# Fields divided 24 to 15 over full banks, sums over positions on VectorE, the context term in one pass

## The reference

```python
def _cin_layer(x0, xk, W, b):
    out = jnp.einsum('bhd,bmd,shm->bsd', xk, x0, W) + b[None, :, None]
    return jax.nn.relu(out)
e = jnp.stack([tbl_0[ids[:, 0]], ..., tbl_38[ids[:, 38]]], axis=1)
x1 = _cin_layer(e, e, W1, b1)          # (1024, 128, 16)
x2 = _cin_layer(e, x1, W2, b2)         # (1024, 128, 16)
z = jnp.concatenate([x1.sum(axis=-1), x2.sum(axis=-1)], axis=-1)
h = jnp.concatenate([z, dense_ctx], axis=1)          # 128 + 128 + 16 = 272
h = jnp.maximum(h @ W_top1 + b_top1, 0.0)            # 512
h = jnp.maximum(h @ W_top2 + b_top2, 0.0)            # 256
y = h @ W_top3
```

## Time and profile before

| | us |
|---|---|
| median of 3 runs | 1210.94 (1210.28 to 1210.98) |
| the profiled execution | 1209.32 |
| its span | 1207.3 |
| TensorE busy | 1162.2 |
| VectorE busy | 1075.3 |
| GpSimd busy | 900.6 |
| ScalarE busy | 692.3 |

### The profile page before, as it was taken

The page is one execution under the profiler, slowest core; times in us unless marked ns, Lnnn a source line. Parts: engine busy times, 40 slices in busy tenths (PEclk is TensorE's granted clock), DMA queues, the critical chain, the costliest instruction groups (busy, mean ns, idle before and its releaser), DMA issues.

```text
span 1207.3 us, 18938 instructions
## 1 busy us (share of the span) xinstructions
PE 1162.2 (96%) x4952; PEld 898.9 (74%) x4952; DVE 1075.3 (89%) x3811; ACT 692.3 (57%) x2177; POOL 900.6 (75%) x930
## 2 busy tenths in 40 slices
PE   3897999999999999999999999999999999999998
PEld 2575777777777777777777677777778777777766
DVE  4476899999999999999999779999999999999966
ACT  3554565656666556666565555566666566656432
POOL 7898998888888888888887676888876454645432
PEclk9998999999999999999999999999999999999998
DMA  5111111111111111111111100111110000000000
GB/s 180 8 7 7 7 8 6 7 6 7 6 7 8 7 6 7 6 6 7 7 7 6 6 5 5 7 7 7 7 6 2 1 1 1 1 1 1 1 1 1
DMA packets 170249, 11.58 MB, mean 10 GB/s; under 512 B 163630, under 2 KB 169262, under 8 KB 170013
## 3 DMA queue, kind: packets, MB, share of 16 engines
q1 hardware_dynamic: 159901, 7.73, 7.5%
q0 software_dynamic: 10240, 2.64, 2.8%
HBM read 7.92 MB, written 0.00 MB: 7 GB/s over the span
## 4 chain that ended last, share of the span: by engine, by line
PE 59%; DVE 16%; ACT 12%; issue 6%; POOL 6%; DMA 0%; POOLq 0%; DVEq 0%; ACTq 0%; SPq 0%
PE ps L881 16%; PE ps L882 15%; DVE acc L769 15%; PE ps L885 14%; ACT fy L552 9%; POOL looked L422 4%; PE ps L914 3%; PE ps L837 2%; ACT ps L585 2%; ACT zh L584 1%; PE ps L850 1%; PE ps L851 1%; PE ps L853 1%; PE ps L825 1%; POOL fsum L431 1%
## 5 line engine op out<-in xcount | busy, mean ns | idle before, releaser
L769 DVE SCALAR_TENSOR_TENSOR acc<-ps,e,acc 128x128 f32<-128x128 f32 x3186 | 846.9, 342 | 76.6 <-PE ps L885 70.6
L431 POOL TENSOR_TENSOR fy<-fy 128x512 f32<-128x512 f32 (+1 forms) x256 | 403.0, 1574 | 204.7 <-ACT fy L552 196.3
L881 PE MATMUL ps<-w2h,x1h 128*128 128x512 f32 (+1 forms) x1280 | 523.3, 409 | 21.2 <-ACT fy L552 9.9
L882 PE MATMUL ps<-w2l,x1h 128*128 128x512 f32 (+1 forms) x1280 | 496.3, 388 | 0.0
L885 PE MATMUL ps<-w2h,x1l 128*128 128x512 f32 (+1 forms) x1280 | 495.5, 387 | 0.4 <-DVE x1l L721 0.4
L552 ACT ACTIVATE fy<-ps,e 128x128 f32<-128x128 f32 x1536 | 415.8, 387 | 83.0 <-PE ps L885 82.9
L422 POOL DMA_INDIRECT looked<-in_table,rows x320 | 311.6, 974 | 58.3 <-POOL fy L431 23.4
L881 PEld LDWEIGHTS ps<-w2h,x1h 128*128 128x128 f32 x1280 | 241.5, 189 | 125.9 <-DVE acc L769 33.9
L885 PEld LDWEIGHTS ps<-w2h,x1l 128*128 128x128 f32 x1280 | 241.1, 188 | 49.6 <-DVE x1l L721 0.9
L882 PEld LDWEIGHTS ps<-w2l,x1h 128*128 128x128 f32 x1280 | 241.7, 189 | 43.7 <-issue 4.7
L584 ACT ACTIVATE zh<-ps 128x512 fp32r<-128x512 f32 x168 | 103.7, 617 | 247.2 <-PE ps L837 243.2
(11 more groups left out here) (87 smaller groups left out, 624.4 us busy)
## 6 DMA issues: line engine op xcount, KB each, us to landing
e<-looked SPq DMA_DIRECT2D x360, 5.0 KB, 1.9
looked<-in_table,rows POOLq DMA_INDIRECT x320, 2.4
e<-looked SPq DMA_DIRECT2D x120, 4.5 KB, 1.9
w_st<-in_w SPq DMA_DIRECT2D x1, 1728.0 KB, 10.1
wt_sb<-in_wt SPq DMA_DIRECT2D x2, 512.0 KB, 4.1
w_st<-in_w SPq DMA_DIRECT2D x1, 768.0 KB, 5.9
w_sb<-in_w1a SPq DMA_DIRECT2D x1, 448.0 KB, 3.2
w1b_sb<-in_w1b SPq DMA_DIRECT2D x1, 448.0 KB, 3.9
```

The source lines that it names most:

```text
L431: nc.gpsimd.tensor_tensor(out, a, b, ALU.add).then_inc(s_fsum, 1)
L769: nc.vector.scalar_tensor_tensor(acc[:, sub, :] if m < fields("D", last)[-1] else y, y, emb(p, sub, m), acc[:, sub, :] if m else fsum[:, p ...
L881: nc.tensor.matmul(y, x1h[:, t % 2, at], w2h[:, cols], start=True, stop=False)
L882: nc.tensor.matmul(y, x1h[:, t % 2, at], w2l[:, cols], start=False, stop=False)
```

## The change

VectorE gets 24 fields in six full banks, ScalarE 15 in four banks, the last with three fields. The ten slots of a pair become D A D D A D D A D A. GpSimd's adds of a pair go from six of 256, 1024, 512, 512, 512 and 256 elements per partition to six of 256, 1024, 1024, 768, 512 and 256. The sum over positions becomes one VectorE instruction per tile, behind `first_layer_low`. The context's term gets its high and low parts stacked on 80 rows, so that one matmul of the fast fp32 form takes the place of one in plain fp32; ScalarE and VectorE prepare the parts once. Tiles 4 and 5 join those whose first layer is unsplit (SOON), pairs 4 to 6 those that add `fsum` at their end (LATE), fewer lookups are issued in pairs 0 to 5, and `e_hl` has four places instead of eight.

```diff
-SOON = 4
+SOON = 6
-MA = 12
+MA = 15
-ORDER = "DDADDADDAD"
+ORDER = "DADDADDADA"
-LATE = 4
+LATE = 7
-ADDS_PER_PAIR = A_BANKS + 3
-LAST_ADDS = 4
+ADDS_PER_PAIR = A_BANKS + 2
+LAST_ADDS = 2
...
 def lookups(p):
-    return 7 if p < 6 else 6
+    return 6 if p == 0 or p >= 4 else 5
 def high_slots(p):
-    return (6, 7) if p == 0 else (0, 1) if SPLIT_IN[p] < SOON else (3, 6)
+    return (6, 7) if p == 0 else (4, 5) if p == 2 else (1, 4) if SPLIT_IN[p] < SOON else (3, 6)
...
-        P1_OPS = 4
+        P1_OPS = 1
...
+                def middle_fields(p, j):
+                    added(p, j, j, fy[:, p % 2, :, 0:4, :], fy[:, p % 2, :, 0:4, :], fy[:, p % 2, :, MB * j:MB * (j + 1), :])
+                def last_fields(p):
+                    added(p, 3, 3, fy[:, p % 2, :, 0:3, :], fy[:, p % 2, :, 0:3, :], fy[:, p % 2, :, 12:MA, :])
+                def four_to_two(p):
+                    added(p, 4, 3, fy[:, p % 2, :, 0:2, :], fy[:, p % 2, :, 0:2, :], fy[:, p % 2, :, 2:4, :])
...
-                    added(p, 5, 2, fsum[:, p % 2, :, :], fy[:, p % 2, :, 0, :], fy[:, p % 2, :, 1, :])
+                    added(p, 5, 3, fsum[:, p % 2, :, :], fy[:, p % 2, :, 0, :], fy[:, p % 2, :, 1, :])
...
+                    if p == 2:
                         low_parts(nc.gpsimd, mine)
                     if then < PAIRS:
-                        four_to_two(then, 2, 1, 0)
+                        middle_fields(then, 1)
+                    look_ahead(1)
...
+                def context_low():
+                    rows = slice(CTX_ROWS[1], CTX_ROWS[1] + CTX)
+                    dve.wait_ge(s_ctxh, 1)
+                    nc.vector.tensor_tensor(ctx_r[rows, :], ctx_sb[rows, :], ctx_r[rows, :], ALU.subtract).then_inc(s_ctxl, 1)
...
+                def position_sum(t):
+                    nc.vector.tensor_reduce(p1[:, t * BT:(t + 1) * BT], x1[:, t % 2, :].rearrange("p (x r) -> p r x", r=BT),
+                                            mybir.AxisListType.X, ALU.add).then_inc(s_p1, 1)
...
                             first_layer_low(p // 2 + 1)
+                            position_sum(p // 2 + 1)
...
-                                 (wt1c_sb[:, f], ctx_sb[:, lo:hi])]
+                                 (wt1c_r[:, f], ctx_r[:, lo:hi])]
```

More of the change, by code:

```diff
@@ L18 @@
 CTX = 16
+CTX_ROWS = (0, 32, 64)
+CTX_K = CTX_ROWS[-1] + CTX
 F1, F2 = 512, 256
@@ L98, in bank_order @@
     slots = [[("A", 0, 0), ("D", 0, 0), ("A", 0, 1), ("D", 0, 1), ("A", 0, 2)]]
-    first = (("D", 0, 2), ("D", 0, 3), ("A", 1, 0), ("D", 0, 4), ("D", 0, 5), ("A", 1, 1), ("D", 0, 6), ("A", 1, 2), ("A", 2, 0))
-    slots += [[bank] for bank in first] + [[]]
+    slots += [[("D", 0, 2)], [("A", 0, 3)], [("D", 0, 3)], [("A", 1, 0)], [("D", 0, 4)], [("A", 1, 1)], [("D", 0, 5)], [("A", 1, 2)],
+              [("A", 1, 3)], [("A", 2, 0)]]
     for p in range(1, PAIRS):
@@ L245, in cin_tower @@
         prod = sb("prod", [P, LOOKED, ZP * DT])
-        e_hl = sb("e_hl", [P, LOOKED, P, DT])
+        e_hl = sb("e_hl", [P, HELD, P, DT])
         x0t = sb("x0t", [P, 2, N], F32R)
@@ L463, in last_sum @@
                     nc.gpsimd.tensor_tensor(fy[:, h, :, 0:2, :], fy[:, h, :, 0:2, :], fy[:, h, :, 2:4, :], ALU.add).then_inc(s_fsum, 1)
-                    pool.wait_ge(s_fy, last_count(1))
+                    pool.wait_ge(s_stt, stt_count(p - 1, 0))
                     pool.wait_ge(s_fsum, n + 1)
[L466 to L470, removed]
-                    nc.gpsimd.tensor_tensor(fsum[:, h, :, :], fy[:, h, :, 0, :], fy[:, h, :, 1, :], ALU.add).then_inc(s_fsum, 1)
[L473 to L481, removed]
+                    nc.gpsimd.tensor_tensor(fsum[:, h, :, :], fy[:, h, :, 0, :], fy[:, h, :, 1, :], ALU.add).then_inc(s_fsum, 1)
                 pool.wait_ge(s_rows, 1)
@@ L531, in _ @@
                         whole_sum(then)
-                    if p % 2 == 0 and p // 2 + 1 < TILES:
-                        position_sum(p // 2 + 1)
                     look_ahead(1)
@@ L618, in products_high, with context_high @@
                     for row in (ZH, ZW):
-                        nc.scalar.activation(e_hl[:, t % LOOKED, row:row + ZP, :].bitcast(F32R), src, ACT.Copy).then_inc(s_eh, 1)
+                        nc.scalar.activation(e_hl[:, t % HELD, row:row + ZP, :].bitcast(F32R), src, ACT.Copy).then_inc(s_eh, 1)
+                def context_high():
+                    act.wait_ge(s_mlpw, 16 * len(mlp_weights))
+                    nc.scalar.activation(ctx_r[:], ctx_sb[:], ACT.Copy).then_inc(s_ctxh, 1)
+                    nc.scalar.activation(wt1c_r[:], wt1c_sb[:], ACT.Copy).then_inc(s_ctxh, 1)
                 def sums_turned(t):
@@ L717, in square_low, with context_weights_low @@
                     nc.vector.tensor_tensor(zl[:, k % 2, :], ps[:, BK_T, :], zh[:, k % 2, :], ALU.subtract).then_inc(s_zl, 1)
+                def context_low():
+                    rows = slice(CTX_ROWS[1], CTX_ROWS[1] + CTX)
+                    dve.wait_ge(s_ctxh, 1)
+                    nc.vector.tensor_tensor(ctx_r[rows, :], ctx_sb[rows, :], ctx_r[rows, :], ALU.subtract).then_inc(s_ctxl, 1)
+                def context_weights_low():
+                    rows = slice(CTX_ROWS[2], CTX_ROWS[2] + CTX)
+                    dve.wait_ge(s_ctxh, 2)
+                    nc.vector.tensor_tensor(wt1c_r[rows, :], wt1c_sb[rows, :], wt1c_r[rows, :], ALU.subtract).then_inc(s_ctxl, 1)
                 def first_layer_low(t):
@@ L825, in turn @@
                         mm = nc.tensor.transpose(ps[:, BK_T, d * P:(d + 1) * P],
[L826 removed]
+                                                 e_hl[:, t % HELD, :, d], ident_sb[:])
                     mm.then_inc(s_full, 1)
@@ L957, in _ @@
                     nc.tensor.matmul(ps[:, TAIL_1[c], 0:n], wt1_sb[:, 0, f], p1[:, lo:hi], start=True, stop=False)
-                    nc.tensor.matmul(ps[:, TAIL_1[c], 0:n], wt1c_sb[:, f], ctx_sb[:, lo:hi], start=False, stop=False)
+                    nc.tensor.matmul(ps[:, TAIL_1[c], 0:n], wt1c_r[:, f], ctx_r[:, lo:hi], start=False, stop=False)
                 sums(TILES - 1)
@@ L1025 @@
     first_row = np.repeat(first_row.reshape(LOOKUPS, Q).T, BT, axis=0)
+    wt1c, ctx_t = np.zeros((CTX_K, F1), np.float32), np.zeros((CTX_K, B), np.float32)
+    for row in CTX_ROWS:
+        wt1c[row:row + CTX], ctx_t[row:row + CTX] = x["W_top1"][2 * S:], x["dense_ctx"].T
     arrays = {
```

62 lines of the change are left out of this document (33 added, 29 removed).

## The result

The changed kernel takes **1283.09 us** (median of four runs, 1282.56 to 1284.29), beside 1210.96 for the kernel before: a ratio of 1.0597 (95% interval 1.0579 to 1.0615). The forecast was 1243, at most 1258. The direction was right, the size was not: the loss is 72 us, where 32 were forecast.

The account below looks back on a forecast made before the run. VectorE and TensorE were both taken as near the bound, with a loop through GpSimd's adds closing after the change. 1209.3 + 42 + 0.5 - 7 - 2.3 - 1.2 = 1241.3, median 1.6 above: 1243 us; range 1208 to 1258.

Parts of the forecast that it names:

- The loop: Slot 3 to slot 3 through GpSimd's adds, `fsum` and VectorE's first bank: tiles of 37.4 us, +53 - 11 = +42.
- fixed part: Loop's share outside TensorE's slots 3 to 7: A bank, ScalarE, GpSimd 6.17, VectorE 2.16, hand-overs; 11.6 us a pair.
- the late add: Even pair's add before the 768 add, its bank drained late: next add starts at 10.9 instead of 10.4, 0.5 us.
- four of seven: Small network's steps at tile 17 that fill the loop's wait; the loop grows by 8 only, not 19: -11.
- Late tiles: Tiles without lookups: a 1.3 us wait in the even pair gives 34.65 a tile against 34.56; +0.5 in all.
- The term sized 0.65: VectorE's reduction over positions, one instruction a tile: 0.65 us, between 0 and 1.4.
- Early pairs: TensorE's 7.44 us standstill in pair 2 shrinks: 9 back, 2 paid for tiles 4 and 5; -7, between -10 and 0.
- Context: Eight plain fp32 products become one pass each: -2.3 in the late tiles, another 2.5 inside the loop's sum.
- Tail: The last add waited for seven fields on ScalarE; four fields in slot 1 are now early: -1.2 us.
- VectorE's relief going to TensorE: Rival: the sums arrive in time, tiles of 34.7 or at best 33.4 us, 1160 to 1192 in all; 15%.
- The loop closed only in part: Rival: the 768 add is cheap (1.30) and the even pair's lag absent: 1221, down to 1209; 12%.
- The clock rival: Rival: each wait of some 2 us at slot 3 draws a stretch at 1.2 GHz, 70 more, 1313; 3%.

Follow-up runs that it names:

- the context's trial: Kernel before with only the context's term in one pass of the fast fp32 form (`e_hl` in four places): 1203.16 us, ratio 0.9947.
- the three edits: Changed kernel, last three adds without lookups between them, `x1l` behind VectorE's third bank, sum over positions at the even pair's end: 1203.24 us, 0.9948.
- the fastest version: Changed kernel with the three edits, TensorE's sums in slot 3 instead of 5, and the last square's low part behind the pair's last bank: 1196.34 us, 0.9890.
- the order of slots: Changed kernel with ORDER = DADDADADDA, fourth A bank in slot 6: 1253.88 us alone, 1229.2 with the three edits.
- the late `fsum`: Changed kernel with LATE = 62, so pairs up to 61 add `fsum` at their end: 1266.72 us, ratio 1.0477.
- the early copy: TensorE's sums of the tile before in slot 3 instead of 5: 1287.76 us on the changed kernel, 1202.15 with the three edits.

## Why the prediction was wrong in size

**The loop (+42, measured +68).** The mechanism and its fixed part were right: 6.15 for GpSimd's chain, odd pairs 17.99. What failed is the step "in an even one three matmuls with the transposes 1.09, two matmuls 0.46, the sums 0.25: 7.3". It gave TensorE's work between slots 3 and 7 and no wait in it. Measured it is 8.77, and two waits stand there: line 866 waits for `x1l`, and line 859 for ScalarE's copy of the sums. The front said that `x1l` "stood in the same place, behind the fourth D bank". By D banks that is true; by slots it is one later, since the fourth D bank moved from slot 4 to slot 5, next to the step that needs `x1l`. So 19 ordinary tiles between pairs 7 and 49 grew by 67.6 us, 3.56 each instead of 2.5, which is 20 of the 26 missed. Of the 1.06 that such a tile is too long on average, putting `x1l` ahead gave back 0.6. With it away the fourth bank still comes some 0.2 later than the late add would let it, by the wait for the copy. The context's parts, priced at 0, are another 0.1: they make the two tiles of pairs 16 to 19 longer by 2.0 together. The last 0.2 was not taken apart. The four network pairs (34 to 37) are the rest: they grew by 0.6 instead of shrinking by 6. In the context's trial they shrank by 4.0 alone, so the closed loop ate that, and its growth with the network is 89.7 - 4 x 19.1 = 13.3 over the ordinary pairs, not 8. By this the step "four of seven" that fill the wait counted too many; which of them don't was not looked into.

**Late tiles (+0.1 each forecast, +1.4 measured).** 35.93 against 34.56. The place of `x1l` is 0.76 of it and the reduction 0.46 by their trials; with both away, 34.86. The term sized 0.65 measured 1.09. The Trainium skill ("VectorE: DVE Perf Modes", rules for kernel authors) calls tensor_reduce the slowest operation of VectorE and advises to consider restructuring it on a hot path: the trace agrees, 1.09 by its record against 0.68 for the subtraction of as many elements.

**Early pairs (-7, measured -0.2).** The standstill of 7.44 us went: pair 2 fell from 26.23 to 19.03 us, the -9 nearly met. It was paid back by pairs 4 and 5, +3.4 (forecast 2), by pair 0, +2.5, and by a start 1.8 later. The reduction's place is 6 of it (its trial). Why pair 0 is longer was not settled: counted from the first matmul of the second layer it took between 31 and 43 us in the runs above, with no edit that aimed at it.

**Context (-4.8).** Better than reckoned, and not by its own arithmetic: 6.5 by itself, 4.0 and 3.7 in the two stretches for which 2.5 and 2.3 were taken. A product of 512 columns saved 0.42 and not the 0.62 that 2.5 for four asks.

**Tail (-1.2, measured +2.4).** Wrong in sign, and not for the reason weighed. The last pair too waits for `fsum` at its first bank. TensorE at slot 3 of pair 63, after:

```profile
1261.70 0.80 PE L903 MATMUL ps<-w2h,x1h 128*128 128x512 f32 x1 [2.63 <-DVE acc L786]
1262.30 0.63 PE L904 MATMUL ps<-w2l,x1h 128*128 128x512 f32 x1
```

and the windows ahead of it and behind it, columns as in the earlier trace rows:

```profile
1254.00:1257.30 3.30, 3.30 (x15) 2.44 (x13) 2.57 (x10) 1.14 (x5) 1.94 (x2) 1.00 0.00 0
1261.70:1264.60 2.90, 2.90 (x7) 2.34 (x8) 2.02 (x8) 0.00 (x0) 0.15 (x1) 0.50 0.00 0
```

It stands still for 2.63 us, since VectorE stood for 2.12 at `fsum`, and then runs seven matmuls at 0.50, 1.2 GHz: 0.43 apart instead of 0.23, 1.4 us more. Before, the same bank (1189.61, in the chain of the earlier trace rows behind 1187.40) had waited 0.41. 2.1 + 1.4, less the 1.2 that was gained as forecast (VectorE goes on at once behind its own last bank), are the 2.3 of this pair.

**The rivals.** VectorE's relief going to TensorE (1160 to 1192) did not come in this kernel. With the three edits it takes 1203 and with two more 1196, both with a wait left in the middle. The range's lower end was also added up wrong: 1211 - 42 - 13 is 1156. The loop closed only in part (1221) is refuted: the 768 add took 1.84 (1.85 taken), and the add before it was as late as forecast (its way there adds up to 7.28, not 7.35; measured 7.48), though in the kernel after the fourth bank came later still. The clock rival is refuted where it counted: the tile at 432.07 has a wait of TensorE of 1.47 us in it (438.77) and 1.00 granted. The Trainium skill ("TensorE: Matmul & The Clock Gate", section on a second failure mode) tells of a bf16 kernel in which cycling through PSUM banks with short idles made the clock go up and down. The tiles looked at in the middle don't show it, the last pair shows one fall.

**Where VectorE's relief went.** Nothing of VectorE's 69 us came to the end: in the middle the loop set the pace, behind pair 49 `x1l` and the reduction did. That doesn't show it to be useless. Freed of these, a tile still took 34.80, because TensorE waited elsewhere. Where those waits went too, in the late tiles of the fastest version, a tile took 33.9 against 34.56 before, near the 33.4 reckoned for TensorE's own work. Whether the last two edits would have shortened the kernel before as well was not tried, so how much of these 0.7 us is the relief stays open.

## What to carry to other kernels

Read a loop's length between two slots with every wait of the instructions in between, not their work alone; for each one look up what its operand waits for, and count the producer's place in slots of the waiting engine, since "behind the fourth bank" moves when the banks are reordered. If an engine with spare time in its sum stands in a chain of dependent steps, take the independent work out from between them: moving two lookups was worth 42 us here and cost nothing. A change of several parts is best timed by parts; one of these (the context's term) was worth 6.5 us alone and was hidden under a loss of ten times that. And an edit that opens one wait is worth only what the next one leaves: here the order of slots, the late `fsum` and the early copy each ran into the wait behind.

## What the runs showed of the hardware

- A TENSOR_REDUCE of 512 elements to 32 on VectorE took 1.09 us, 1.00 from its start to the next instruction's (485.29 to 486.29); the subtraction of 512 elements took 0.60 so.
- TensorE kept its 1.00 through an idle stretch of 1.4 us or so in each tile of the middle. After one of 2.63 us in the last pair of the kernel after it ran at 0.50 for seven matmuls. In the fastest version, at the same place, it stood still just as long and kept the pace of 0.23 to 0.35:

```profile
1175.52 0.51 PE L902 MATMUL ps<-w2h,x1h 128*128 128x512 f32 x1 [2.60 <-DVE acc L782]
1175.87 0.40 PE L903 MATMUL ps<-w2l,x1h 128*128 128x512 f32 x1
1176.10 0.40 PE L906 MATMUL ps<-w2h,x1l 128*128 128x512 f32 x1
```

So the length of the last idle stretch alone doesn't tell what the clock will do; what does was not tried here.
- A lookup that GpSimd issues costs its own stream 0.98 us, between an add of 256 elements (0.76) and one of 512 (1.30), though nobody waits for its data there.
